# A new SBUF layout for a two-layer cross-attention kernel: every matmul operand tensor begins at a multiple of 2048 bytes of its partition

## The reference, cut to what matters

```python
def _cross_attention(q_in, kv_in, wq, bq, wk, bk, wv, bv, wo, bo, bias_k, bias_v):
    qh, kh, vh = (q_in @ wq + bq), (kv_in @ wk + bk), (kv_in @ wv + bv)   # each in heads
    kh = concatenate([kh, bias_k], axis=1)          # one learned key and value
    vh = concatenate([vh, bias_v], axis=1)
    weights = softmax(einsum('bqhk,bthk->bhqt', qh, kh) / sqrt(K))
    return einsum('bhqt,bthk->bqhk', weights, vh).reshape(b, q_len, H * K) @ wo + bo

x = x + _cross_attention(_layer_norm(x, ...), ctx, ...)      # layer 1
x = x + _cross_attention(_layer_norm(x, ...), ctx, ...)      # layer 2
h = _layer_norm(x, ln_mlp_scale, ln_mlp_offset)
out = x + gelu(h @ w_fc1 + b_fc1) @ w_fc2 + b_fc2
```

## The kernel before, in words

| product | moving, stationary | columns | matmuls in a turn |
|---|---|---|---|
| scores | k, q | 512 | 24 |
| project_q | h, wq | 512 | 12 |
| project_k | cT, wk | 512 | 24 |
| project_v | wv, cT | 256 | 48 |
| context | pT, v | 256 | 48 |
| unit_output | wo, o | 256 | 24 |

## Time and profile before

### The profile page before, as it was taken

One profiled execution on the slowest core, in us unless ns is written; L12 is line 12 of the kernel. 1 busy time (PEld: TensorE's weight loads), 2 busy tenths in 40 slices (PEclk: granted clock), 3 DMA queues, 4 the chain that ended last, 5 costly groups with the idle time before them and its releaser, 6 DMA issues.

```text
span 497.4 us, 11021 instructions
## 1 busy us (share of the span) xinstructions
PE 489.4 (98%) x3228; PEld 444.8 (89%) x3228; DVE 391.4 (79%) x911; ACT 331.2 (67%) x727; POOL 414.2 (83%) x387
## 2 busy tenths in 40 slices
PE   8999999999999999999999989999999999999997
PEld 6888998998999898999988879989989989999997
DVE  4889878888878878856789868788878888766896
ACT  3677867667776867665486866758676677768541
POOL 4877989989898998996597969989989898999542
DMA  8435886756667676612115776675866566640001
GB/s 278 141 97 174 273 240 204 199 189 194 183 205 196 208 214 190 192 43 65 42 43 194 239 255 169 209 223 179 235 190 193 193 195 186 198 120 1 23 23 42
DMA packets 52901, 82.56 MB, mean 166 GB/s; under 512 B 5882, under 2 KB 33934, under 8 KB 52878
## 3 DMA queue, kind: packets, MB, share of 16 engines
q1 hardware_dynamic: 52878, 82.28, 54.1%
HBM read 53.42 MB, written 28.84 MB: 165 GB/s over the span
## 4 chain that ended last, share of the span: by engine, by line
PE 85%; POOL 4%; issue 3%; DVE 3%; DMA 3%; ACT 1%; SPq 1%; POOLq 0%; ACTq 0%; DVEq 0%
PE ring L1190 62%; PE ps_ctx L1190 10%; PE acc L1190 10%; DMA spill<-blocks 1%; PE ring L1236 1%; POOL probs L422 1%; DMA wf_hi<-spill 1%; DMA probs<-ctx_in 1%; SPq L271 1%; POOL v_lo L415 1%; POOL wf_lo L354 1%; DVE pT_lo L890 0%; PE ring L1545 0%; DVE h_lo L971 0%; PE ring L1273 0%
## 5 line engine op out<-in xcount | busy, mean ns | idle before, releaser
L905 DVE TENSOR_REDUCE row_max<-ring 128x1 f32<-128x512 f32 x112 | 76.1, 688 | 27.4 <-PE ring L1190 27.2
L634 ACT ACTIVATE probs<-ring,shift 128x512 f32<-128x512 f32 x112 | 76.5, 684 | 18.8 <-DVE shift L910 18.6
L415 POOL TENSOR_TENSOR v_lo<-v_sum,v_hi 128x512 fp32r<-128x512 f32 x64 | 83.0, 1299 | 2.7 <-ACT v_hi L584 2.7
L868 DVE STREAM_TRANSPOSE blocks<-probs 128x512 f32<-128x512 f32 x108 | 70.1, 687 | 5.5 <-POOL probs L422 5.2
L422 POOL TENSOR_SCALAR probs<-probs,inv 128x512 f32<-128x512 f32 x80 | 55.6, 702 | 19.8 <-DVE inv L918 19.7
L427 POOL TENSOR_TENSOR pT_lo<-wf_lo,pT_hi 128x1024 fp32r<-128x1024 f32 x28 | 67.1, 2419 | 0.0
L1190 PE MATMUL ring<-pT_lo,v_hi 128*128 128x256 f32 x208 | 58.4, 281 | 0.2 <-DVE pT_lo L890 0.2
L566 ACT ACTIVATE k_hi<-ring,cols 128x512 fp32r<-128x512 f32 x57 | 37.8, 689 | 30.7 <-PE ring L1190 30.6
L1190 PE MATMUL ring<-pT_hi,v_hi 128*128 128x256 f32 x208 | 58.0, 279 | 0.0
L1190 PE MATMUL ring<-pT_hi,v_lo 128*128 128x256 f32 x208 | 58.0, 279 | 0.0
L1190 PE MATMUL ring<-wv_lo,cT_hi 128*128 128x256 f32 x196 | 54.9, 280 | 0.0
(11 more groups left out here) (208 smaller groups left out, 1640.7 us busy)
## 6 DMA issues: line engine op xcount, KB each, us to landing
spill<-blocks SPq DMA_DIRECT2D x54, 512.0 KB, 2.9
wf_lo<-spill SPq DMA_DIRECT2D x112, 128.0 KB, 3.2
wf_hi<-spill SPq DMA_DIRECT2D x104, 128.0 KB, 3.1
wk_raw<-wk_in SPq DMA_DIRECT2D x17, 256.0 KB, 2.8
wq_raw<-wq_in SPq DMA_DIRECT2D x17, 256.0 KB, 3.6
wv_raw<-wv_in SPq DMA_DIRECT2D x16, 256.0 KB, 3.8
vrows<-vrows_in SPq DMA_DIRECT2D x16, 256.0 KB, 4.1
wo_raw<-wo_in SPq DMA_DIRECT2D x16, 256.0 KB, 2.7
```

The costliest lines, as they stand in the source:

```text
L415: pool.tensor_tensor(v_lo[:, 2 * m:2 * m + 2, :], v_sum[:, m % 2, :].rearrange("p (t c) -> p t c", c=PW), v_hi[:, 2 * m:2 * m + 2, :].bitc ...
L634: act.activation(probs[:, u, q, :], ring[S_BANKS[where][QTB * u + q]][:], ACT.Exp, bias=shift[:, u, q:q + 1], scale=SCALE, accum_out=row_s ...
L868: last = dve.transpose(blocks[:, u % 2, :, :, q, :].rearrange("p g c b -> p c g b"), probs[:, u, q, :].rearrange("p (c g b) -> p c g b", g ...
L905: dve.reduce_max(row_max[:, u, q:q + 1], ring[S_BANKS[where][QTB * u + q]][:], AX_X).then_inc(max_done, 1)
```

## The change

The order of the SBUF tensors is written anew. The small ones, and `vbias`, come first; a tensor `filler`, which nothing uses, takes up what is left to the next multiple of 2048 bytes; then come `zeros` and the large tensors, whose sizes are all multiples of 2048; `out_rows` and `ident` go to the end. No shape, no instruction, no wait and no DMA is touched; the order of the work on each engine is the same row by row, but for line numbers that are ten higher.

From the sizes, the start of each tensor that a matmul reads, in bytes past a multiple of 2048 (all slices of them begin a multiple of 512 bytes further on):

| tensors | before | after |
|---|---|---|
| cT_hi, cT_lo, h_hi, h_lo (called group A) | 1792 | 0 |
| wq, wk, wv, wo, each hi and lo (B) | 1984 | 0 |
| q, k, v, each hi and lo (B too: 448 past a multiple of 512, like the weights) | 960 | 0 |
| pT, o, wf1, wf2, each hi and lo (C) | 1152 | 0 |
| zeros | 640 | 0 |
| probs, z_sb (transposes) | 960, 1792 | 0, 0 |
| ident (transposes) | 128 | 1024 |
| head_rows, dim_rows (one transpose each) | 672, 1184 | 160, 672 |

So before, A lies 256 bytes, B 448 and C 128 past a multiple of 512; after, all three lie at 0. All starts of matmul operands but the last row's are multiples of 64 bytes in both.

```diff
@@ -1,3 +1,4 @@
+import math
 from contextlib import ExitStack
 import concourse.bass as bass
@@ -65,13 +66,20 @@
 G_LAG = 6
 WF1_PARTS = FB // PW
 WARM_UP, KEEP_WARM = 5, 2
+SB_FIRST, SB_GRAIN, ROW_BYTES = 16512, 32, 2048
 LOAD = 16
 def build_program(nc, spill, x_in, ctx_in, wq_in, wk_in, wv_in, wo_in, vrows_in, head_rows_in,
                   dim_rows_in, out_rows_in, wf1_in, wf2_in, out):
     with ExitStack() as stack:
+        taken = []
         def sb(name, shape, dt=F32):
+            taken.append(-(-4 * math.prod(shape[1:]) // SB_GRAIN) * SB_GRAIN)
             return stack.enter_context(nc.sbuf_tensor(name, shape, dt))
         def sem(name):
@@ -81,18 +89,29 @@
         ring.append(stack.enter_context(nc.psum_tensor("ps_ctx", [P, 512], F32)))
         acc = [stack.enter_context(nc.psum_tensor(f"acc{i}", [P, 512], F32)) for i in range(2)]
-        ident = sb("ident", [P, P])
-        zeros = sb("zeros", [P, 512], F32R)
         minus_half = sb("minus_half", [P, QT])
         head_rows = sb("head_rows", [P, P])
         dim_rows = sb("dim_rows", [20, P])
         head_cols = sb("head_cols", [P, 4, LAYERS * HEADS])
         step_cols = sb("step_cols", [P, ALL_PAIRS + 2, 3, 2])
         cols = sb("cols", [P, 3, 2])
         dim_cols = sb("dim_cols", [P, 20])
         table_load = sb("table_load", [P, 1])
-        out_rows = sb("out_rows", [P, NORMS, D])
+        bn = sb("bn", [P, QT, 6])
+        mean_var = sb("mean_var", [P, QT, 2])
+        var_eps = sb("var_eps", [P, QT])
+        rstd = sb("rstd", [P, QT])
+        row_max = sb("row_max", [P, NU, QTB])
+        shift = sb("shift", [P, NU, QTB])
+        p_learned = sb("p_learned", [P, NU, QTB])
+        row_sum = sb("row_sum", [P, NU, QTB])
+        total = sb("total", [P, NU, QTB])
+        inv = sb("inv", [P, NU, QTB])
+        vbias = sb("vbias", [P, PW])
+        sb("filler", [P, -(SB_FIRST + sum(taken)) % ROW_BYTES // 4])
+        zeros = sb("zeros", [P, 512], F32R)
         cT_hi = sb("cT_hi", [P, DC, CT * P], F32R)
         cT_lo = sb("cT_lo", [P, DC, CT * P], F32R)
         x_sb = sb("x_sb", [P, QT, D])
@@ -101,10 +120,6 @@
         h_full = sb("h_full", [P, DC, TOK])
         h_hi = sb("h_hi", [P, DC, TOK], F32R)
         h_lo = sb("h_lo", [P, DC, TOK], F32R)
-        bn = sb("bn", [P, QT, 6])
-        mean_var = sb("mean_var", [P, QT, 2])
-        var_eps = sb("var_eps", [P, QT])
-        rstd = sb("rstd", [P, QT])
         wq_raw = sb("wq_raw", [P, DC, PW])
         wk_raw = sb("wk_raw", [P, DC, PW])
         wv_raw = sb("wv_raw", [P, DC, PW])
@@ -114,24 +129,19 @@
         wv_hi, wv_lo = sb("wv_hi", [P, DC, PW], F32R), sb("wv_lo", [P, DC, PW], F32R)
         wo_hi, wo_lo = sb("wo_hi", [P, 2, D], F32R), sb("wo_lo", [P, 2, D], F32R)
         vrows = sb("vrows", [P, 2, PW])
-        vbias = sb("vbias", [P, PW])
         q_hi, q_lo = sb("q_hi", [P, 2, TOK], F32R), sb("q_lo", [P, 2, TOK], F32R)
         k_hi, k_lo = sb("k_hi", [P, 2, CT * P], F32R), sb("k_lo", [P, 2, CT * P], F32R)
         v_sum = sb("v_sum", [P, 2, 2 * PW])
         v_hi, v_lo = sb("v_hi", [P, CT, PW], F32R), sb("v_lo", [P, CT, PW], F32R)
         probs = sb("probs", [P, NU, QTB, CLEN])
-        row_max = sb("row_max", [P, NU, QTB])
-        shift = sb("shift", [P, NU, QTB])
-        p_learned = sb("p_learned", [P, NU, QTB])
-        row_sum = sb("row_sum", [P, NU, QTB])
-        total = sb("total", [P, NU, QTB])
-        inv = sb("inv", [P, NU, QTB])
         blocks = sb("blocks", [P, 2, QB, CTB, QTB, BLK])
         pT_hi, pT_lo = sb("pT_hi", [P, 2, CTB, QLEN], F32R), sb("pT_lo", [P, 2, CTB, QLEN], F32R)
         o_hi, o_lo = sb("o_hi", [P, 2, TOK], F32R), sb("o_lo", [P, 2, TOK], F32R)
         wf_raw = sb("wf_raw", [P, 2, 512])
         wf1_hi, wf1_lo = sb("wf1_hi", [P, DC, FB], F32R), sb("wf1_lo", [P, DC, FB], F32R)
         wf2_hi, wf2_lo = sb("wf2_hi", [P, FT, D], F32R), sb("wf2_lo", [P, FT, D], F32R)
+        out_rows = sb("out_rows", [P, NORMS, D])
+        ident = sb("ident", [P, P])
         wf2_spare = [w[:].bitcast(F32).rearrange("p f d -> p (f d)") for w in (wf2_hi, wf2_lo)]
```

## The result

The changed kernel takes 504.74 us, the kernel before 499.16 beside it. The 504.74 us are the median of four runs of which one took 809.0 us at a granted clock of 0.558; the three others, on which the ratio rests, took 503.66, 503.8 and 505.67. The ratio is 1.010, with a 95% interval of 1.0076 to 1.0124: slower by 1.0%, some 5 us, where 491.5 was forecast. The profiled execution has a span of 503.8 us and took 505.67.

A forecast was written before the change was run, and what follows sets the result against it. TensorE's matmul pitches were taken to bound the kernel. A gain of 10.2 us less 2.7 for settling gave 7.5, so a span of 489.9, plus 1.6 for the median: 491.5 us, range 488.6 to 501.5.

The forecast's parts named there:

- What bounds the kernel: TensorE, busy 489.4 of 497.4 us and without idle time in the loop turns, so time is the sum of matmul pitches.
- Starts of the moving and stationary tensors: All matmuls: equal starts give 113.3 ns at 256 columns and 226.7 at 512, saving 10.2 us at most.
- signs: If right: turn 27.2 to 27.5 us, unit_output, project_v, context 113 to 114 ns, project_k 226.7, hidden layer below 119.
- Settling: Where the column count changes between products, 14 times a turn: 5.5 us lost or nothing; half taken, 2.7 us.
- Other engines, DMAs, filler: Work beside TensorE stays hidden behind it and filler adds no instruction; cost taken as nothing.
- The rule of two ports: TensorE reads moving operand and weights over separate SBUF ports, so layout could not matter; time stays at 499.0 us.
- equal offsets collide at 256 columns: Rival: both reads step on the same place, 256 columns at 119.1 to 120 ns; 500.6 to 508.4 us, chance 0.22.
- no effect: Rival: project_v shows two paces at one pair of starts, so layout changes nothing; 499.0 us, chance 0.20 including a balance.
- The mark set for a collision: Sign in the loop turn that the forecast is wrong: 256 columns at 119 ns and more.

The follow-up runs named there:

- e_classes: The changed kernel with two unused 192-byte gaps, ahead of wq_raw and blocks, restoring the relations of the kernel before at other starts; 499.81 us, ratio 1.0014.
- e_shift: The changed kernel with its filler 192 bytes longer, so all large tensors move together and keep their relations; 506.04 us, ratio 1.0125.
- e_best192: The changed kernel with gaps putting wv, wo, pT and wf2 192 bytes past a multiple of 256, other product operands at 0; 499.08 us, ratio 0.9993.
- e_ring_b: As e_ring_a, but with wv at 0, so project_v's moving tensor begins 64 bytes before its stationary one; 496.93 us, ratio 0.9958.
- micro_next: Constants-only kernel whose starts change from matmul to matmul, making either the own pair or the next one's equal; 116.7 ns in both cases with 64 bytes.
- micro_map: Constants-only kernel, each pair of starts behind six 512-column matmuls at equal starts; at 256 columns 117.8 ns for pair 0, 192 and 113.3 for 192, 256.
- e_ring: The changed kernel with gaps so every product's moving tensor begins 64 bytes past its stationary one modulo 256 (wk 192, cT 256); 498.39 us, ratio 0.9989.
- micro_offsets: Constants-only kernel, 39 pairs of starts, each 12 matmuls of 512 columns, then 24 of 256; equal starts settled at 226.7 and 120.0 ns.
- e_ring_a: As e_ring, but wk at 0, cT at 64 and wv at 128, so only project_v has other starts; 501.76 us, ratio 1.005.

## Why the prediction was wrong, point by point

**What bounds the kernel: right.** The time followed the sum of matmul pitches; the turns in the middle of a layer stayed without idle time in every layout.

**Starts of the moving and stationary tensors: here it failed, in one term.** That the relation of the starts sets the pitch was right (e_classes, e_shift). The step that failed is the price of 256 columns at equal starts. Scores, 512 columns, hold their good pace there, and so the good pace of 256 columns, half as long, was put in for all: 113.3 ns, which the rows of before show at unequal starts only the earlier trace rows. Measured are 120.0 settled and 119.6 with the entries. 2160 x 6.3 ns = 13.6 us covers the whole miss, 504.74 - 491.5 = 13.2. At equal starts 226.7 for 512 columns held, but 512 and 256 are ranked the other way round: of the relations that the products have in these layouts, equal starts give the one its best pace and the other its worst. No row of before had a 256-column product at equal starts, and the prediction said so; the inference across column counts should have been priced as open. Of its signs, project_k at 226.7 and borders without flips came; unit_output, project_v and context at 113 to 114 ns and a hidden layer below 119 did not.

**Settling: right in size, by luck.** Half of 14 changes at 23 ns was taken, 161 ns a turn, since no row told which of two values held. At equal starts it is 7 changes, those from 256 to 512 columns, at 6 x (231.2 - 226.7) = 27 ns: 189 ns. The change the other way costs nothing: the first 256-column matmul is 6 ns shorter than the rest. It is no fixed price of a change either: e_best192 has none. And scores did not hold 226.7 "whatever came ahead": at 122.88 in before six take 1.39 us, 232 each, and don't settle.

**Other engines, DMAs, filler: right**, no cost in the turns read. The profiled execution shows 4% of the chain at spill<-blocks in place of 1%, and its first loop turn takes 28.85 us, 0.7 more than the turns read above. In e_ring_b that turn takes 1.3 us more than the later ones and in e_best192, with the same order of tensors, no more, so I take it for a difference between executions; no run tests that.

**The rule of two ports** (the Trainium skill, "TensorE: Matmul & The Clock Gate", section "Step-by-step: what each phase is for") says that loading weights takes nothing from the running matmul; the prediction drew from it that the layout could not matter, 499.0. The runs contradict what was drawn: moving tensors against each other by gaps alone shifted the time from 0.9958 to 1.0125 of the kernel before. Whether it is the two reads that meet was not shown.

**The rivals.** The one that came is *equal offsets collide at 256 columns*, with a chance of 0.22: its two ends were 119.1 ns (500.6 us) and 120 ns with 232.5 for 512 columns (508.4 us, a turn of 28.35); measured 120.0, 229.8 on the mean and 28.14. Its reason, that a weight load lies beside nearly all of a 256-column matmul, was not shown; micro_next leaves it open. The "no effect" rival argued from one pair of starts at two paces. That observation was right, and micro_map and e_ring show it again at other starts; it only didn't carry over to equal starts, where one pace is left. The mark set for a collision, 256 columns at 119 and more, is what the trace shows, and the range, up to 501.5, cut off the case that came.

## What to carry to other kernels

Where TensorE has no idle time, read the pitch of each kind of matmul from start to start, and try the relation of moving to stationary start (modulo 256 bytes) as a tuning knob: here it moved the time by 1.7%, from 0.9958 to 1.0125 of the kernel before, and starting all operands alike gave the slowest layouts of those tried. A pace seen at one column count did not carry over to another; measure the pair in a kernel of constants, and then in the real order of products, since the pace can depend on the product ahead.

## What the runs showed of the hardware

- float32r matmuls with 256 columns have lasting paces of 113.3, 117.8 and 120.0 ns, and others between, at the same granted clock of 1.00; with 512 columns 226.7, 229 and 233. Which are open to a product hangs on the difference of its two tensors' starts modulo 256 bytes (micro_offsets, e_classes, e_shift).
- At a difference of 64 or 192 two paces last for 256 columns, 113.3 and 117.8, and the matmuls ahead choose (the pairs 0, 192 and 192, 256 in micro_offsets and micro_map); at 0 the mean is 120.0 each time. With 512 columns the pair 192, 256 has two as well: 233.3 in micro_offsets, 229.0 in micro_map.
- A difference of 4 bytes was the slowest of those tried: 123.3 and 236.8 ns.
- Not settled: which reads meet (micro_next), what in the matmuls ahead decides the pace, and why e_ring_b's project_v brings the good pace back while e_ring_a's, at the same distance on the other side, does not.
